# Moving one sum of weights and the order of the split weights in a fused attention and feed-forward kernel

## What is computed

```python
x = L0_attn_hidden_states            # (4, 512, 1024)
xn = _layernorm(x)
x + attn(xn, w_qkv, w_o) + ffn(xn, W, b, A, B, gate_w, gate_b)

def attn(h, w_qkv, w_o):             # 32 heads of 128, 8 key and value heads
    q, k, v = split(h @ w_qkv)
    scores = einsum('bqhgd,bkhd->bhgqk', q, k) * 128 ** -0.5
    bias = where(rel >= 0, -slopes * sqrt(max(rel, 0)), -inf)
    p = softmax(scores + bias)
    return einsum('bhgqk,bkhd->bqhgd', p, v).reshape(B, S, 4096) @ w_o

def ffn(h, W, b, A, B, gate_w, gate_b):
    # h @ W.T + b, plus a low-rank term whose rank (8, 16, 32 or 64)
    # and weight a softmax gate chooses for each token
```

## Time and profile before

| | |
|---|---|
| median of three runs | 2504.72 us |
| the profiled execution | 2503.76 us |
| its span | 2502.0 us |
| TensorE (PE) busy | 2413.1 us, 96% |
| VectorE (DVE) busy | 1506.7 us, 60% |
| ScalarE (ACT) busy | 1385.0 us, 55% |
| GpSimd (POOL) busy | 780.6 us, 31% |
| 16 DMA engines, mean | 182 GB/s |

### The profile page before, as it was taken

How to read it: one execution, slowest core, us unless ns; L and a number is a source line. 1 busy time by engine, 2 the same in 40 slices (tenths; PEclk the granted TensorE clock), 3 DMA queues, 4 the chain that set the end, 5 groups by cost and what they waited for, 6 DMA issues and landing times.

```text
span 2502.0 us, 35041 instructions
## 1 busy us (share of the span) xinstructions
PE 2413.1 (96%) x12128; PEld 2051.0 (82%) x12128; DVE 1506.7 (60%) x2817; ACT 1385.0 (55%) x3075; POOL 780.6 (31%) x1029
## 2 busy tenths in 40 slices
PE   5999999997899999999799999999999999999999
PEld 4787888886778888888788888888888888888887
DVE  6657455565655555555566666666666676666665
ACT  4532133334533223333777777778777677777764
POOL 3211000000320000000343645546345464454644
PEclk9999999999999999999999999999999999999999
DMA  4536344546344544544755565655656556555543
GB/s 149 189 127 217 138 153 167 202 168 219 111 147 173 189 144 175 203 152 156 269 185 185 188 221 180 220 187 186 215 198 208 182 195 216 192 204 203 185 169 127
DMA packets 118320, 455.95 MB, mean 182 GB/s; under 512 B 11945, under 2 KB 12089, under 8 KB 109184
## 3 DMA queue, kind: packets, MB, share of 16 engines
q1 hardware_dynamic: 86176, 334.37, 38.7%
q0 software_dynamic: 31968, 119.33, 13.7%
HBM read 276.96 MB, written 176.69 MB: 181 GB/s over the span
## 4 chain that ended last, share of the span: by engine, by line
PE 90%; DVE 5%; ACT 2%; issue 1%; DMA 1%; POOL 1%; DVEq 0%; SPq 0%; ACTq 0%; POOLq 0%
PE ps L656 28%; PE ps L658 28%; PE ps L657 28%; PE ps L843 5%; DVE stats L1151 1%; ACT rows L934 1%; DVE pt_lo L1137 0%; DVE w_lo L1137 0%; DVE probs L1374 0%; ACT res_hi L905 0%; DMA lora_lo<-lora_s 0%; DVE wo L1137 0%; DVE res_a L1227 0%; PE ps L738 0%; DVE res_b L1137 0%
## 5 line engine op out<-in xcount | busy, mean ns | idle before, releaser
L905 ACT ACTIVATE w_hi<-raw 128x1024 fp32r<-128x1024 f32 x196 | 207.0, 1059 | 560.0 <-PE ps L658 440.0
L1137 DVE TENSOR_TENSOR w_lo<-raw,w_hi 128x1024 fp32r<-128x1024 f32 x196 | 239.2, 1224 | 358.0 <-ACT w_hi L905 357.7
L1405 DVE TENSOR_TENSOR acc<-ps,acc 128x512 f32<-128x512 f32 x448 | 298.2, 687 | 235.2 <-issue 210.8
L656 PE MATMUL ps<-x_hi,w_hi 128*128 128x512 f32 x1120 | 436.5, 390 | 0.0
L657 PE MATMUL ps<-x_lo,w_hi 128*128 128x512 f32 x1120 | 435.9, 389 | 0.0
L658 PE MATMUL ps<-x_hi,w_lo 128*128 128x512 f32 x1120 | 435.8, 389 | 0.0
L1045 ACT ACTIVATE probs<-probs,neg_max 128x512 f32<-128x512 f32 (+3 forms) x512 | 284.1, 567 | 176.5 <-DVE neg_max L1374 176.4
L656 PE MATMUL ps<-wo,op_hi 128*128 128x512 f32 x896 | 362.5, 405 | 18.4 <-DVE wo L1137 18.4
L658 PE MATMUL ps<-wo,op_lo 128*128 128x512 f32 x896 | 353.6, 395 | 0.0
L657 PE MATMUL ps<-wo,op_hi 128*128 128x512 f32 x896 | 352.2, 393 | 0.0
L1374 DVE CUSTOM_DVE_ANT_0 probs<-ps,bias 128x512 f32<-128x512 f32 (+3 forms) x512 | 220.5, 486 | 96.9 <-PE ps L658 93.4
(11 more groups left out here) (158 smaller groups left out, 4780.3 us busy)
## 6 DMA issues: line engine op xcount, KB each, us to landing
raw<-w_all SPq DMA_DIRECT2D x70, 1024.0 KB, 5.2
q<-qk_s SPq DMA_DIRECT2D x128, 512.0 KB, 3.9
acc<-acc_s SPq DMA_DIRECT2D x128, 512.0 KB, 5.2
acc_s<-acc SPq DMA_DIRECT2D x112, 512.0 KB, 7.8
qk_s<-res_hi POOLq DMA_DIRECT2D x40, 1024.0 KB, 4.6
qk_s<-res_a POOLq DMA_DIRECT2D x20, 1024.0 KB, 9.1
qk_s<-res_b POOLq DMA_DIRECT2D x20, 1024.0 KB, 5.2
k<-qk_s SPq DMA_DIRECT2D x32, 512.0 KB, 3.6
```

What stands on the lines that cost most here:

```text
L656: pe.matmul(to, st_hi, mv_hi, start=start, stop=False, skip_group_check=True)
L905: nc.scalar.activation(to, source, ACT.Copy).then_inc(signal, 1)
L1137: nc.vector.tensor_tensor(to, source, high.bitcast(F32), ALU.subtract).then_inc(signal, 1)
L1405: nc.vector.tensor_tensor(to, fill[f % 2][:, :], to, ALU.add).then_inc(s_acc, 1)
```

## The change

The tables change; no instruction is added or taken away.

```diff
-WO_SUMS_IN = {6: (4,), 8: (2, 3), 9: (5,)}
-WO_ORDER = (0, 1, 4, 3, 2, 6, 5)
-HIGHS_FIRST = {9: (4,), 10: (6,)}
-HIGHS_LAST = {6: (0,), 7: (1,), 9: (3, 2), 10: (5,)}
-LOWS_EARLY = {9: (4,), 10: (2,)}
-LOWS_MIDDLE = {10: (6,)}
-LOWS_LAST = {6: (0,), 7: (1,), 9: (3,), 10: (5,)}
+WO_SUMS_IN = {6: (4,), 8: (2, 3, 5)}
+WO_ORDER = (0, 1, 6, 4, 2, 3, 5)
+HIGHS_FIRST = {9: (4,)}
+HIGHS_LAST = {6: (0,), 7: (1,), 8: (6,), 9: (2, 3), 10: (5,)}
+LOWS_EARLY = {9: (4,), 10: (3,)}
+LOWS_LAST = {6: (0,), 7: (1,), 8: (6,), 9: (2,), 10: (5,)}
...
                 if n < UNITS:
                     inverses(n)
-                for f in todo[1:3]:
-                    add_fill(*f)
-                for part in making(n, LOWS_MIDDLE):
-                    out_split(*part)
-                for f in todo[3:]:
+                for f in todo[1:]:
                     add_fill(*f)
                 for part in making(n, LOWS_LAST):
                     out_split(*part)
```

## The result

| | before | after |
|---|---|---|
| median, 21 runs each on the same chip | 2503.29 us | 2509.63 us |
| lowest and highest | 2498.74, 2508.20 | 2507.26, 2514.22 |
| ratio of the medians, 95% interval | | 1.0025 [1.0019, 1.0031] |
| span of the profiled execution | 2502.0 us | 2507.8 us |

The kernel became slower by 6.3 us. The forecast had the sign, the mechanism and the range; it had said 2515.

What follows compares the result with a forecast made beforehand. TensorE was taken as the bound (90% of the last-ending chain). Seven groups would lose 7 x (4.6 + 0.8) = 37.8 us instead of 25.2, +12.6, with group 0 -1.5: from 2503.8 to 2515 us, range 2502 to 2530.

Steps and rivals of the forecast that it cites:

- The wait for `wo` goes: TensorE at place 10, fill 2: the 2.18 us wait for the low of step 2 goes, new waits of 4.6 us come.
- GpSimd's queue: Sum 5 at place 8 stands ahead of place 9's out_sums; ScalarE's third op_hi and all behind it come 4.2 us later.
- The collisions: VectorE's lows 6 and 4 beside GpSimd's sums 2 and 5: each costs the sum about 1.0 us.
- Group 0: First group: sum 5's excess falls (-2.9 us), high 6 costs ScalarE-paced units 1.0 to 1.6; together -1.5 us.
- The clock: TensorE at half clock in the seven later units at place 10: half a stretch, 0.8 us each, between 0 and 3.1.
- Its own lower edge: Low end of the forecast's own range: 4.1 us idle a unit and no half clock, +1.5 us, 2505 us.
- two half-clock stretches a group: Rival: TensorE idles 4.6 us and loses 3.1 us to the clock in each of seven groups; 2531 us, chance 0.12.
- The lows and sums pass each other: Rival: lows 6 and 4 cost GpSimd's sums nothing, so the queue runs only 2.3 us late; 2492 to 2500 us, chance 0.12.
- Nothing takes the place: Rival: the wait for low 2 goes and no other wait comes at place 10; 2476 us, chance 0.06.
- the 28.7 us: The most the change can win: eight units at place 10 take 112.10 us, eight of 10.43 would take 83.44.

Runs made afterwards that it cites:

- The second pair of traces: The kernels before and after, unchanged, each run once more to look at the clock: 2504.00 us (before) and 2510.49 us (after).
- the order alone: Changed kernel with sum 5 put back to place 9, so only the new order of highs and lows: 2524.66 us, 1.0084 to the kernel before.
- The kernel with both orders: Changed kernel with sum 2 ahead of place 8's out_lows, sum 5 behind place 9's first out_low, low 2 behind place 10's maxima: 2477.80 us.
- sum 5 cut: Changed kernel with sum 5 reduced to 8 of its 1024 columns, making step 5's weights wrong: 2490.09 us, 0.9945 to the kernel before.

## Why the prediction was right, and where it was not

**The wait for `wo` goes**: right; the line is gone. The three waits in its place were to cost 2.2 (`op_lo`), 1.2 (`at_raw`), 1.05 (`acc`) and 0.15 (`pt_lo`), 4.6 a unit. The brackets read 1.90, 0.91, 0.91 and none. The prediction counted from start to start, and so counted the unit of group 2 reads 2.1, 1.1, 1.2 and 0.1, 4.54 in all; the mean of seven is 4.58 (15.01 - 10.43). One term came out by luck. The addition was to be done "near 1418.7", but the prediction's own terms give 1414.6 + 1.6 + 1.65 + 0.68 = 1418.5 at the most, and 1418.1 with 1.2 for the low of 2: a wait of 0.4 to 0.8, not 1.05. The low of 2 took 1.79, longer than the 1.2 to 1.6 allowed, because it met the next `out_sum`, and that made the slip good.

**GpSimd's queue**: right. Sum 2 went from 2.83 to 3.82, sum 5 took 3.81. ScalarE waits 4.09 us for `op_raw`, where about 4 was expected, and its third `op_hi` starts 2.42 us after the start of place 10, where it started 1.77 ahead of it: 4.2 later, the figure of the prediction.

**The collisions**: right, and shown by taking the lows away: 0.95 and 0.96 of a unit for 1.0 each. The third, low 2 beside `out_sum`, is in the term above.

**Group 0**: right as far as two pairs of traces can tell. The unit at place 10 fell by 3.0 (predicted 2.9), and the units ahead of it grew by 1.3 (predicted 1.4): -1.7 for -1.5. The -1.0 in the spans has 0.7 from the later start of the stage in it. The second pair of traces gives -2.8 counted from the stage's start, with 6.8 us of half clock in the unit of the kernel before; how much of the 1.3 is high 6 and how much the queue, no run separates.

**The clock**: this is the term that was mis-sized. The step read "I take half a stretch, 0.8", between nothing and 3.1. It measured 0: one unit of seven had a half-clock stretch, and that unit is as long as the others (14.98, 14.97). 7 x 0.8 = 5.6 us is all but 0.1 of the difference between +12.6 and +6.87. Two things were wrong in it. It counted on half clock in the seven units, and this came in one of them: the longest piece of idle time is 1.9 us instead of 2.18, and at place 10 the stretches came more often with a longer piece than with more idle time in all (3.7 us in three pieces, 2 of 12 units; 3.7 in one piece, 7 of 7). And it charged half of a stretch's 1.57: behind the first wait ScalarE and VectorE pace the unit, not TensorE, and slower products only fill the waits that follow. Of this the prediction said the right sentence ("slower products partly fill what would be waiting") and then halved the price where the whole had to go.

Its own lower edge, 4.1 us idle and no half clock (2505), had the clock right and the idle time too low. With 4.6 and no half clock it would have given 7 x 4.6 - 25.2 - 1.5 = +5.5: 2509.3.

**The rivals**: two half-clock stretches a group did not come here; with the order alone they did in three of seven. "The lows and sums pass each other" is refuted by the durations. "Nothing takes the place" named its own condition, that GpSimd's delay be under 0.6 us or sum 2 start three us earlier. The kernel with both orders meets both: against place 10, its second `out_sum` starts 0.67 us earlier than in the kernel before (3.82 and 3.15 ahead of it), and its sum 2, at 1393.22, 3.6 us earlier. It ends at 2477.8, where 2476 had been worked out for that case. So the 28.7 us were there to be won (the eight units are 28.6 shorter, the whole 26.5); what stood between the change and them was the place of two sums and one low.

What stays open is what makes a wait of 2.18 us be followed by a half-clock stretch in one group and not in the next. The runs give shares, not a rule.

## What to carry to other kernels

Before moving an operation ahead in an in-order queue, list what stands behind it and who waits for that: here a sum that nobody needed soon was put ahead of one with 0.64 us of slack, for which ScalarE waited, and the whole gain went. With that sum four operations further down, and one low behind the maxima instead of ahead of them, 28 us came back (2509.63 to 2481.57). Changes to a schedule that depend on each other (a sum, and the low written over its source) have to be costed together: alone the two parts here cost 4.0 and 2.8 us a unit, together 1.0. And a half-clock stretch, or any slowing of the busiest engine, is to be charged only where that engine paces the work; behind a wait with more waits to come it may be free, as it was here for stretches of 3.4 us (those of 6.8 cost 0.4 to 0.5).

## What the runs showed of the hardware

- A low of 1024 columns on VectorE (two inputs in SBUF) beside a sum in four pieces of 256 on GpSimd costs the sum 0.96 to 0.99 us each time (2.83 to 3.81), and the low itself takes 1.42 to 1.64 instead of 1.22. It made no difference which sum the low fell on.
- A stop of TensorE costs some 0.3 us beyond the idle time in its row: 0.30 with one stop (kernel before, 12.91 with a bracket of 2.18), 0.55 with two (sum 5 cut, 12.21 with 0.26 and 0.97), 0.82 with three (after, 14.97). Part of it is how the rows show a stream (0.39 long, 0.23 apart).
- Idle time of 3.7 us in one piece was followed by half clock in 7 of 7 units, the same in three pieces (the longest 1.9) in 2 of 12, and in pieces of up to 1.3 us in 0 of 28, all at place 10. There, cutting a wait into pieces went with fewer stretches even where their sum stayed. At the start of the stage two pieces of under 1.8 us close together were enough in 5 of 14 traces.
- A half-clock stretch of 3.4 us made the unit 1.59 us longer where no other wait followed (12.88, 14.47), and no longer where further waits for ScalarE and VectorE did (15.01 and 14.97).
